# Causal attention block on one core: scores masked by an identity matmul, maxima taken over mask rows, four operand slots, a new order

## The reference

```python
y = _layernorm(x, ln_w, ln_b)
q, k, v = (einsum('bsd,hde->bhse', y, w) for w in (wq, wk, wv))
scores = einsum('bhse,bhte->bhst', q, k) / sqrt(8) + causal      # -inf above the diagonal
attn = einsum('bhst,bhte->bshe', softmax(scores), v).reshape(32, 256, 128)
x = _layernorm(x + (attn @ wo + x))                    # here 2*x + attn @ wo, called z
w_low = up_aux @ (lora_up @ (lora_down @ down_aux))
x = _layernorm(x + (x @ (W + w_low).T + b))            # the second addend's sum is called f
```

## Time and profile before

| | |
|---|---|
| median of 3 runs | 674.22 us |
| the profiled execution, span | 678.9 us |
| PE busy, share of the span | 80% |
| DVE | 76% |
| ACT | 60% |
| POOL | 52% |
| moved by DMA | 69.35 MB, mean 102 GB/s |

### The profile page before, as it was taken

One profiled execution on the slowest core, in us unless ns is written; L12 is line 12 of the kernel. 1 busy time (PEld: TensorE's weight loads), 2 busy tenths in 40 slices (PEclk: granted clock), 3 DMA queues, 4 the chain that ended last, 5 costly groups with the idle time before them and its releaser, 6 DMA issues.

```text
span 678.9 us, 18688 instructions
## 1 busy us (share of the span) xinstructions
PE 543.5 (80%) x5192; PEld 327.1 (48%) x5192; DVE 515.3 (76%) x2959; ACT 407.1 (60%) x1025; POOL 352.9 (52%) x494
## 2 busy tenths in 40 slices
PE   1267788798878889898888887888888888798893
PEld 0124345455545545555555554555555554455442
DVE  6166568888768878888888886789788877778764
ACT  0214446666656667776766675577576655666683
POOL 7404345646546546655655654555456554644352
PEclk9999779999889999989999997999899988989896
DMA  1343344544334554444444444545344435534210
GB/s 33 92 104 92 74 114 119 127 104 121 99 80 108 125 127 126 118 111 120 112 114 113 112 121 90 126 111 118 100 117 115 109 90 127 117 88 104 53 32 25
DMA packets 70891, 69.35 MB, mean 102 GB/s; under 512 B 6955, under 2 KB 66146, under 8 KB 66146
## 3 DMA queue, kind: packets, MB, share of 16 engines
q1 hardware_dynamic: 70818, 68.61, 41.0%
HBM read 47.07 MB, written 20.99 MB: 100 GB/s over the span
## 4 chain that ended last, share of the span: by engine, by line
DMA 31%; PE 29%; DVE 16%; issue 10%; POOL 5%; SPq 5%; ACT 3%; POOLq 0%; DVEq 0%; ACTq 0%
DMA kx<-k_rows 14%; DMA qx<-mT 13%; DVE max_bank L576 6%; PE pv_bank L637 5%; DMA q_rows<-parts 4%; PE bank L669 4%; DVE rowmax L576 4%; PE score_bank L621 4%; PE max_bank L610 3%; PE max_bank L609 3%; PE bank L670 3%; POOL parts L329 2%; SPq L236 2%; PE bank L645 2%; POOL probs L310 2%
## 5 line engine op out<-in xcount | busy, mean ns | idle before, releaser
L576 DVE CUSTOM_DVE_ANT_0 max_bank<-max_bank,causal 128x128 f32<-128x128 f32 (+1 forms) x1024 | 341.2, 377 | 109.4 <-PE max_bank L610 101.8
L437 ACT ACTIVATE probs<-score_bank 128x384 f32<-128x384 f32 x512 | 244.6, 493 | 204.0 <-PE score_bank L622 202.4
L609 PE MATMUL max_bank<-kx,qx 128*128 128x128 bf16 x512 | 118.8, 232 | 99.6 <-DMA kx<-k_rows 67.3
L310 POOL TENSOR_SCALAR_AFFINE_SELECT probs<-probs 128x1024 f32<-128x1024 f32 x128 | 140.2, 1095 | 62.2 <-ACT probs L437 60.6
L316 POOL TENSOR_TENSOR rs<-ve,power 128x2 f32<-128x2 f32 x96 | 67.5, 703 | 154.9 <-DVE ve L478 151.6
L621 PE MATMUL score_bank<-qx,kx 128*128 128x256 bf16 x512 | 145.1, 284 | 3.6 <-DMA qx<-mT 2.2
L610 PE MATMUL max_bank<-kx,qx 128*128 128x256 bf16 x512 | 147.3, 288 | 0.0
L576 DVE DVE_READ_ACCUMULATOR2_ANT rowmax<- 128x1 f32 x1024 | 143.6, 140 | 0.2
L637 PE MATMUL pv_bank<-probs,v_ext 128*32 128x256 f32 (+1 forms) x2048 | 138.9, 344 | 0.8 <-POOL probs L310 0.8
L609 PEld LDWEIGHTS max_bank<-kx,qx 128*128 128x128 bf16 x512 | 51.4, 100 | 153.5 <-DVE rowmax L576 66.5
L622 PE MATMUL score_bank<-qx,kx 128*128 128x128 bf16 x512 | 115.5, 226 | 0.0
(11 more groups left out here) (69 smaller groups left out, 738.0 us busy)
## 6 DMA issues: line engine op xcount, KB each, us to landing
kx<-k_rows SPq DMA_DIRECT2D x96, 192.0 KB
qx<-q_rows SPq DMA_DIRECT2D x64, 192.0 KB
qx<-q_rows SPq DMA_DIRECT2D x32, 208.0 KB
q_rows<-parts SPq DMA_DIRECT2D x32, 192.0 KB, 2.1
k_rows<-parts SPq DMA_DIRECT2D x32, 192.0 KB, 2.4
xa<-in_x SPq DMA_DIRECT2D x32, 128.0 KB, 2.2
k_rows<-parts SPq DMA_DIRECT2D x32, 128.0 KB, 2.3
xr<-in_x SPq DMA_DIRECT2D x32, 128.0 KB, 2.3
```

The source lines that it names most:

```text
L310: pool.affine_select(out=t, in_=t, compare_op=ALU.is_ge, fill=0.0, base=0, pattern=[[0, GROUP * NB], [1, P]], channel_multiplier=-1)\
L437: act.activation(probs[:, h, 0:PW], score_bank[h % 2][:, 0:PW], ACT.Exp, scale=SCALE)\
L576: ins = dve.tensor_tensor_reduce(max_bank[h % 2][:, a:b], max_bank[h % 2][:, a:b], causal[:, SEQ - (b - a):SEQ], 1.0, LOWEST, ALU.add, ALU ...
L609: pe.matmul(bank[:, 0:P], q[:, h, 0:P], k[:, h, 0:P], start=True, stop=True)
```

## The change

- **Score mask.** `future` holds 0 where a key is allowed and -2^54 where it is not. For each head PE first multiplies it by the identity into the score bank (256 columns, bfloat16), and the two score matmuls accumulate on it. The exponential gives 0 there. POOL's four masks of `probs` per step go. q carries a factor 2^-72, which ACT's `scale` takes out.
- **Maxima over mask rows.** The free rows of `qx` and `kx` (74 to 127) hold constants whose products are 0 for allowed keys and very negative for future ones. The diagonal blocks of the maxima are contracted over all 128 rows, the rest over 74, always 128 columns at a time. DVE takes plain maxima (`tensor_reduce`) of a whole bank: 12 *units* per step (four heads x 128, or two heads x 256), in slots `UNIT_AT`.
- **Slots and order.** Four slots of `qx`, `kx`, `v_ext`, `xa` instead of three; three score banks, one `pv_bank`. The parts of `it+3` are made and stored in step `it` and spread in step `it+1`; the scores of a batch begin at slot 8 of its step (`LAG`) and end at slot 7 of the next. All 16 heads' maxima go through one split, transpose, copy and pair of transfers. Heads are multiplied with v in halves: two groups of four accumulate in the same bank by windows of `v_ext`, and each half has one copy, transpose and division. The loop takes four steps per pass.
- **Elementwise work moved.** x1 from ACT to DVE, y from ACT to POOL, the addition of eps from DVE to POOL; the shifts `nm2`, `nm3` and POOL's `x1b` go (the identity is added to the weight, the bias to f).
- **Start.** The q, k weights come by ACT's queue; the low-rank product moves to step -3; DVE and ACT fill the mask rows of each slot before its first use, POOL `v_ext`.

```diff
+LAG = 8
+UNITS = 12
+UNIT_AT = {u * 4 // 3: u for u in range(UNITS)}
+SCORE_BANK = [0, 1, 2] * 4 + [0, 1, 2, 1]
-RING = 3
+RING = 4
@@ SP, step
-                    max_rows(it, 1, 0)
+                    max_rows(it, 0)
                 if it.runs(2):
-                    sp.wait_ge(s_expand, it.done(1, EXPAND))
-                    sp.wait_ge(s_p3, it.done(2))
-                    store_parts(it)
-                    sp.wait_ge(s_score[HEADS - 1], it.done(-1))
-                    expand(it)
-                if it.runs(1):
-                    max_rows(it, 0, 1)
+                    if first_use(it, 2):
+                        sp.wait_ge(s_qmask, it.base + 3)
+                        sp.wait_ge(s_kmask, it.base + 3)
+                    sp.wait_ge(s_score[HEADS - 1], it.done(-2))
+                    expand(it, 2)
...
+                if it.runs(3):
+                    sp.wait_ge(s_expand, it.done(2, EXPAND))
+                    sp.wait_ge(s_p3, it.done(3))
+                    store_parts()
@@ POOL
-                pool.affine_select(out=t, in_=t, compare_op=ALU.is_ge, fill=0.0, base=0,
-                                   pattern=[[0, GROUP * NB], [1, P]], channel_multiplier=-1)\
-                    .then_inc(s_mask[group], 1)
@@ DVE
+            def fill_mask(to, mask, signal):
+                dve.tensor_copy(to[64:P, :, :].rearrange("p h (n s) -> p (h n) s", s=P),
+                                mask[64:P, :].rearrange("p (o s) -> p o s", o=1).to_broadcast([64, HEADS * NB, P]))\
+                    .then_inc(signal, 1)
+            def row_max(it, unit):
+                quad, kind = unit // 3, unit % 3
+                if unit == 0:
+                    dve.wait_ge(s_mp2, it.done(0))
+                dve.wait_ge(s_mscore[unit], it.done(1))
+                b = max_bank[unit % 2]
...
+                dve.tensor_reduce(to, of, AX.X, ALU.max).then_inc(s_mread[unit], 1)
-                        for n, (a, b) in enumerate(((0, P), (P, PW))):
-                            ins = dve.tensor_tensor_reduce(max_bank[h % 2][:, a:b], max_bank[h % 2][:, a:b],
-                                                           causal[:, SEQ - (b - a):SEQ], 1.0, LOWEST, ALU.add, ALU.max,
-                                                           rowmax[half][:, n, c:c + 1])
@@ ACT, side
+                if s == 5 and it.runs(3):
+                    act.wait_ge(s_xT, it.done(3))
+                    act.wait_ge(s_v, it.done(2))
+                    act.activation(yT[:, :], bank6[:, 0:SEQ], ACT.Identity, bias=lnb_s[:, :], scale=lnw_s[:, :])\
+                        .then_inc(s_yT, 1)
@@ PE
-                pe.matmul(bank[:, 0:P], q[:, h, 0:P], k[:, h, 0:P], start=True, stop=True)
-                pe.matmul(bank[:, P:PW], q[:, h, P:SEQ], k[:, h, 0:SEQ],
-                          start=True, stop=True).then_inc(s_mscore[h], 1)
+                if kind == 0:
+                    for g in range(GROUP):
+                        h = quad * GROUP + g
+                        ins = pe.matmul(b[:, g * P:g * P + P], q[:, h, 0:P], k[:, h, 0:P], start=True, stop=True)
+                else:
+                    for g in range(2):
+                        h = quad * GROUP + 2 * (kind - 1) + g
+                        pe.matmul(b[:, g * SEQ:g * SEQ + P], q[:, h, P:SEQ], k[:, h, P:SEQ], start=True, stop=True)
+                        ins = pe.matmul(b[:, g * SEQ + P:g * SEQ + SEQ], q[0:SCORE_ROWS, h, P:SEQ],
+                                        k[0:SCORE_ROWS, h, 0:P], start=True, stop=True)
@@ PE, scores: bank h % 2 before
-                pe.matmul(bank[:, 0:SEQ], k[:, h, 0:P], q[:, h, :], start=True, stop=True)
-                pe.matmul(bank[:, SEQ:PW], k[:, h, P:SEQ], q[:, h, P:SEQ],
-                          start=True, stop=True).then_inc(s_score[h], 1)
+                last = last_in_bank(h)
+                pe.wait_ge(s_exp[last % HEADS], it.done(offset if last >= 0 else offset - 1))
+                b = score_bank[SCORE_BANK[h]]
+                pe.matmul(b[:, :].rearrange("p (c s) -> p c s", s=SEQ)[:, :, 0:P], ident_b[:, :], future[:, :, :],
+                          start=True, stop=False, skip_group_check=True)
+                pe.matmul(b[:, 0:SEQ], k[0:SCORE_ROWS, i, 0:P], q[0:SCORE_ROWS, i, :], start=False, stop=True,
+                          skip_group_check=True)
+                pe.matmul(b[:, SEQ:PW], k[0:SCORE_ROWS, i, P:SEQ], q[0:SCORE_ROWS, i, P:SEQ],
+                          start=False, stop=True, skip_group_check=True).then_inc(s_score[h], 1)
```

More of the change, by code:

```diff
@@ L341, in step @@
[L341 to L354 removed]
+            make_masks()
@@ L441, in _ @@
-            act.wait_ge(s_w, N_W)
+            def step(it):
+                for s in range(HEADS):
+                    h, offset = (s - LAG) % HEADS, 0 if s >= LAG else -1
+                    if it.runs(offset):
+                        if h % GROUP == 0:
+                            act.wait_ge(s_pv[h // GROUP], it.done(offset - 1))
+                        act.wait_ge(s_score[h], it.done(offset))
+                        act.activation(probs[:, h, 0:PW], score_bank[SCORE_BANK[h]][:, 0:PW], ACT.Exp, scale=SCALE / Q_SCALE)\
+                            .then_inc(s_exp[h], 1)
+                    side(it, s)
@@ new lines, in pv @@
+            def pv(it, group, offset):
+                r, half, sub = it.ring(offset), group // 2, group % 2
+                if sub == 0:
+                    pe.wait_ge(s_pvs[1 - half], it.done(offset if half else offset - 1))
+                if group == 0:
+                    pe.wait_ge(s_vx, it.done(offset))
+                pe.wait_ge(s_exp[GROUP * group + GROUP - 1], it.done(offset))
+                window = slice(0, VW) if sub else slice(SUB, SUB + VW)
+                for n in range(NB):
+                    for g in range(GROUP):
+                        h = GROUP * group + g
+                        ins = pe.matmul(pv_bank[VW * g:VW * g + VW, n * P:SEQ], v_ext[r][:, n, head(h), window],
+                                        probs[:, h, 0:SEQ] if n == 0 else probs[:, h, SEQ:PW],
+                                        start=(n == 0 and sub == 0), stop=(n == NB - 1 and sub == 1),
+                                        skip_group_check=True)
+                ins.then_inc(s_pv[group], 1)
@@ L654, in max_transpose, with transpose2 @@
+            def transpose2(to, source, signal):
+                for n in range(NB):
+                    ins = pe.transpose(to[:, n * P:n * P + P], source(n), ident[:, :])
+                ins.then_inc(signal, 1)
+            def max_transpose(it, offset):
+                pe.wait_ge(s_mp2, it.done(offset))
                 for n in range(NB):
[L655 to L656 removed]
@@ new lines, in side @@
+                if s == 15 and it.runs(0):
+                    pv(it, 0, 0)
+            def step(it):
+                for s in range(HEADS):
+                    if s in UNIT_AT and it.runs(1):
+                        max_scores(it, UNIT_AT[s])
+                    h, offset = (s - LAG) % HEADS, 0 if s >= LAG else -1
+                    if it.runs(offset):
+                        scores(it, h, offset)
+                    side(it, s)
+                if it.static and it.base == FIRST + 1:
+                    low_rank()
```

709 lines of the change are left out of this document (340 added, 369 removed).

## The result

The changed kernel takes 548.0 us (median of 4 runs, 547.4 to 549.0), the kernel before 674.4 us on the same chip (median of 4). The ratio is 0.812, with a 95% interval of 0.807 to 0.816. The forecast was 598 us with a range of 568 to 634: the direction was right, the gain was 50 us larger than forecast and lies outside the range.

A forecast was written before the change was run, and what follows sets the result against it. The prediction took PE's own work to bound the changed kernel: head 48 + start 5 + 32 steps x 16.6 + tail 19 = 603 us of span, less 4.7 for the median, 598 us; range 568 to 634.

The forecast's parts named there:

- PE's work becomes 15.7 + 0.9 = 16.6 us: PE's step: busy time 15.7 us plus the change's net 0.9 gives 16.6 us, which sets the step.
- The turns from score matmuls to other kinds and back: PE's step: eight turns become about three, two groups of narrow maxima transposes become one, about -0.5 us.
- the two pairs of transposes: PE's step: two pairs of pv_s transposes fewer at 0.27 us each, -0.54 us.
- Start extra: Beginning of the steps: last fills in step 0 and PE's lower starting clock cost 5 us more (2 to 10).
- 5 us under PE: DVE's step: 11.1 us of work, 5 us below PE's, so half a microsecond of reduction error costs nothing.
- It ends near 13.7 of 16.6: 2.9 us of cover: Spreading of kx: done near 13.7 us of a 16.6 us step, 2.9 us before it is needed.
- ACT's wait of slot 5: ACT waits for the transposed xhat; PE meets this at slot 9, the tightest place, 0.3 to 0.5 us.
- Late transfers: Rival, chance 0.08: spreading takes 12 to 13 us, PE waits again for kx, step about 17.9, 640 us.
- weight loads: Rival, chance 0.05: PE's 128-column matmuls run at their loads' pace, +2.6 us a step, 681 us.
- accumulation: Rival, chance 0.05: PE waits when adding to a bank just written, 4.3 us a step, 736 us.
- In-order waits: Rival, chance 0.17: waits on ACT, DVE and PE cost several tenths each, step 17.4, 624 us.
- Less than the sum: Rival, chance 0.08: PE's work nearer 15.8 than 16.6 us and a short head, 570 us.

The follow-up runs named there:

- experiment 9: Kernel before with identity matmul and plain maxima of twelve units (no causal mask): ratio 0.972; with the short spread of k too: 0.891, step 16.53 us.
- experiment 10: Products with v joined into sixteens in the kernel before: ratio 1.047; split into eight pieces in the changed kernel: 576.9 us, ratio 0.862.
- experiment 1: Changed kernel without the identity matmul, future keys not masked: 525.5 us, ratio 0.780, step 14.28 us.
- experiment 8: Kernel before with the identity matmul in place of POOL's four masks: ratio 0.989; with only one of three kx transfers too: 0.913.
- experiment 5: DVE's reductions over half of each bank: changed kernel 538.8 us; changed kernel with score mask from the mask rows, no identity matmul, 508.0 us.
- experiment 7: Kernel before with one transfer instead of three spreading k into kx, the rest left out: 608.1 us, ratio 0.914.
- experiment 4: Changed kernel with two score banks instead of three: 586.3 us, ratio 0.871, step 16.33 us.

## Why the prediction was wrong, step by step

**What failed: "PE's work becomes 15.7 + 0.9 = 16.6 us".** By starts PE's work is 14.4 us, and 0.5 us of waits make the step 14.95. That PE bounds the step was right. Its work was priced 2.2 us too high, in three terms of the sum:

| PE's time by starts, us a step | old order (experiment 9) | changed kernel |
|---|---|---|
| identity and score matmuls | 5.33 | 4.88, of it 0.22 wait |
| maxima | 2.75 | 3.13, of it 0.30 wait |
| products with v | 3.71 | 3.02 |
| transposes of `pv_s` | 1.10 | 0.58 |
| transposes of the maxima | 0.42 | 0.22 |
| other float32 matmuls | 3.23 | 3.12 |
| step | 16.53 | 14.95 |

- The 15.7 is PE's busy time in windows in which PE also waited. The forecast called it "generous by some tenths". Experiment 9 gives 14.77: it was 0.93 too high. A busy time counts the drawn-out ends before each wait (in the kernel before, the maximum that waited for `kx` at 342.85 starts 1.46 us after the matmul before it instead of 0.11; of these 1.35 us the profile shows 1.19 as idle); a sum of starts does not, and the rows for it were at hand.
- The joining of the products with v was put at nothing, without a reason. By starts, sixteen products are 0.79 instead of 0.93 us, and thirty-two 1.44 (312.22 to 313.66) instead of 1.86: together 3.02 instead of 3.72, -0.70.
- The turns from score matmuls to other kinds and back, with the transposes of the maxima, were put at -0.5. The lines for scores, transposes of the maxima and other matmuls, less the wait, come to -1.0. Splitting the products again (experiment 10) takes back 0.95 of both terms together.

The identity matmul (+1.76 of PE's time) and the two pairs of transposes (-0.52) agree with their rows, though the first costs the kernel only 0.67 a step (experiment 1); the maxima are +0.1 instead of +0.2. In the other direction, the waits had no term of their own: they were to come out of the generous tenths. So 16.6 - 0.9 - 0.7 - 0.5 - 0.1 + 0.5 = 14.9, against 14.95 measured.

**The sum of the span.** Forecast 603, measured 546.5. Steps: 32 x (14.95 - 16.6) = -52.8. Start extra: the scores of the first batch take 19.06 us, 4 over the rest, and the turns of the loop add about 4, but those of the last four batches take 14.65, 13.52, 12.35 and 9.9, in steps that lack stages; net -2.2 instead of +5, so -7.2. Head 48.4 against 48, tail 21.9 against 19: +0.4 and +2.9. Sum -56.7. The median of the runs lies 1.5 us above the profiled span and not 4.7 below it: +6.2. The forecast took the 4.7 from the one profiled execution of the kernel before as if it held for any kernel; in the experiments the median lies between 0.9 us below and 8.8 us above the span of the profiled execution.

**DVE's side.** The reduction was right: 0.68 busy, forecast 0.6 to 0.69. DVE's step is 12.1, not 11.1, and "5 us under PE" was really 2.8. The 0.387 us of a `ve` was a mean of short ones and of some lengthened beside POOL (experiment 8). That the error didn't matter holds for this kernel (experiment 5), not for one with 1.8 us less on PE (experiments 1 and 5).

**Transfers.** "It ends near 13.7 of 16.6: 2.9 us of cover": all has landed near 13.5 of 14.95. The end was right, and the cover was smaller because the step was. The loss at `kx` was named as one of three; experiment 7 makes it 58 us with its clock, of 126. That the clock stays at the upper level was right: 1.00 in the middle, 0.959 over the run.

**Waits.** ACT's wait of slot 5 was expected to cost PE 0.3 to 0.5 us a step, at slot 9. It is there, once a step (9.8 us, 30 times), here 0.83 before the q products of slot 10:

```profile
188.86 0.10 PEld L641 LDWEIGHTS score_bank<-future,ident_b 128*128 128x128 bf16 x1 [0.32 <-ACT probs L449]
```

That this is the tightest place experiment 4 confirms: with two banks the wait for `probs` becomes the bound.

**The rivals.** Late transfers, weight loads and accumulation didn't occur: 4.0 us, 0.06 and 0.11 in the rows above. In-order waits are there, 0.5 us a step, and were outweighed. The page's 81 ns for 128 columns with a load (the Trainium skill, TensorE: Matmul & The Clock Gate, "Back-to-back issue gap") is not what this trace shows: 300.07 to 300.13 and their neighbours are 0.055 to 0.07. "Less than the sum", 570, had the right direction with 0.08, and still had PE's work at 15.8.

## What to carry to other kernels

Price an in-order engine by the starts of consecutive instructions over a whole step, and add the waits apart: here busy time said 15.7 where the work was 14.7 to 14.8. Where an arrangement joins or splits runs of narrow float32 products, compare the whole run from its first start to the next instruction, and not only the turn into it. And with two engines and a transfer close to each other (kx, DVE at 16.6, PE at 16.5), what one of them costs depends on what else is still there: the identity matmul cost nothing in the old kernel and 0.02 to 0.03 of ratio in the new one, and halved reductions the other way round gave nothing until it was gone.

## What the runs showed of the hardware

- Narrow products of float32 (32 columns of the array, 128 or 256 streamed): eight take 0.36 and 0.57 us before another kind of matmul, sixteen 0.79, thirty-two 1.44. Each break costs about 0.14 us (0.93 - 0.79) beyond the turn of 0.09 (0.15 - 0.06).
- A bfloat16 matmul that adds to the bank that the one before it has just written starts 0.11 us after it, as without.
- At the turn of a loop with 93 to 95 instructions a step on DVE, DVE stands 2.4 us (experiment 7); with 40 a step in the same loop (experiment 9) and with 34 in the changed kernel's no such row is left. Why is not shown.
- DVE's `ve` (128x2) takes 0.165 us on the mean without POOL's masks and 0.387 with them (experiment 8); every `ve` and `nm` over 0.4 us ran beside a long POOL instruction.
